# A mixture-of-experts stage on one Trainium2 core: the first expert product turned, its weights streamed per slot

## The chip, the cores and the metric

The kernel runs on one core of one Trainium2 chip, in one launch. The metric is the device time in microseconds; three runs of the kernel before took 3836.7 to 3844.87 us, with a median of 3841.38 us. A core has five engines that run their own instruction streams and meet at semaphores: PE (TensorE, matrix products), DVE (VectorE), ACT (ScalarE), POOL (GpSimd) and SP (SyncE, which here only issues DMAs). PE accumulates into PSUM, eight banks of 512 float32 per partition (`bank0` to `bank7`); everything else lies in SBUF, 128 partitions wide.

## The reference, cut to what matters

One layer of a graph transformer on 3125 nodes of 256 features, all in float32: three rounds of a relational graph convolution over 103,125 edges with 8 relations, a linear attention beside it, and a feed-forward part in which a router picks 2 of 8 experts for each node. The change is in the last part:

```python
xn = (xt - mu) * jax.lax.rsqrt(var + LN_EPS)
xe = xn[None, :, :] * ln_g[:, None, :] + ln_b[:, None, :]
h = jax.nn.gelu(jnp.einsum('end,edh->enh', xe, W1) + b1[:, None, :], approximate=False)
y = jnp.einsum('enh,ehd->end', h, W2) + b2[:, None, :]
sel = jnp.take_along_axis(jnp.transpose(y, (1, 0, 2)), top_idx[:, :, None], axis=1)
out = (weights[:, :, None] * sel).sum(axis=1)
```

W1 is 8 x 256 x 1024 (8 MB), W2 is 8 x 1024 x 256 (8 MB). The kernel doesn't compute all eight experts for each node: it sorts the 6250 chosen (node, expert) pairs by expert into 56 slots of 128 rows, each of one expert, and computes each slot once.

## The kernel before, in words

**Layers.** Three graph layers follow each other. In each, POOL issues one indirect DMA per tile of 128 edges (`gather`, L473, 806 a layer), which brings 128 rows of 256 features from `rows_dram` into one of 22 gather places, taken in two halves of 11. PE multiplies each tile with a one-hot matrix (L1293), DVE adds the result up (L987), and PE multiplies what was collected for 128 nodes with the relation weights (L1236). The one-hot matrices of 11 tiles are made by one DVE instruction (L958), and ACT copies the indices of the next 11 gathers into a ring (L554) once PE has finished the 11 tiles that used those places before: the 23rd gather of a layer waits for the first 11 tiles of PE.

**Start of the last layer.** DVE and PE wait there for `ffw_in`, the small parameters of the experts: SP loads `ln_g`, `ln_b` (L376, L377; one DMA per expert and vector, each of 256 single words), the router's weights and `b1` (L380). DVE then fills `bsel` (L948, L950) and makes the first one-hot matrices. After these loads SP starts on the part of W1 whose place in `arena` isn't in use (L389).

**Preparing the slots.** After the last layer DVE computes the routing: where each pair goes (`pos`) and which expert each slot has (`slot_exp`). POOL then scatters the normed rows into `xs_dram`, one indirect DMA for each tile of 128 nodes and choice (L507, 50 in all). Meanwhile all of W1 and W2 is brought into SBUF (L389, L391), PE works out `ln_b @ W1` for all experts (`fold`, L1387), DVE adds it to `b1` (L1112), and ACT and DVE multiply W1 by `ln_g` in place (L735, L1114, eight instructions of 128 x 1024 each). `b1` goes out to `b1_dram`.

**Slots.** A slot s on PE, in the order in which it is written (`slot`, L1415): four plus four transposes of the Gelu rows (L1423); `hidden` of slot s+1, four products of 128 x 512 with the rows as stationary side (L1411); two transposes of the rows of slot s+2 (L1430); the second product of slot s, eight products of 128 x 256 (L1438). Around it DVE adds the bias to the hidden rows (L1123), ACT applies Gelu (L749), DVE and ACT copy the turned rows back (L1130, L756), ACT copies the turned rows of the next input back (L740), and DVE adds `b2` (L1135). SP reads the slot's expert number, loads `b1` and `b2` of that expert into all 128 partitions (L405, 512 KB; L406, 128 KB), loads the rows (L401) and stores the result (L422). In float32 each product is two passes on PE, each with its own weight load, so the trace counts 8, 16 and 8 matmuls for L1411, L1438 and L1423 (a transpose is one pass).

**Combining.** When all slots are stored, POOL gathers the results back (L518) and DVE adds them to the nodes (L1152).

## Time and profile before

| | us |
|---|---|
| median of 3 runs | 3841.38 |
| the profiled execution | 3845.77 |
| its span, first to last instruction | 3844.0 |
| three graph layers, up to the last end of a layer on DVE | 3183.6 |
| routing, from there to the first scatter | 21.6 |
| scatter, to the first load of rows | 70.6 |
| slots, from the first load of rows to the end of the last second product | 491.4 |
| combining, to the end | 76.8 |

The profile is of one execution, on the only core. Each engine's work is shown by its busy time; an engine's idle time costs something only where that engine is the one that the others wait for. On the right of a line of the timeline stands how long the engine was idle before it, and what ended that. `DMA` rows give the time from issue to landing. Where a product has more than one form, the views leave its shape out.

### The profile page before, as it was taken

Reading aid. Unit: us, or ns where it says so; the run is one execution under the profiler, and the core shown is the slowest. Engines: PE = TensorE matmul, PEld = TensorE weight load, DVE = VectorE, ACT = ScalarE, POOL = GpSimd, SP = SyncE. Lnnn points to the kernel's source line nnn. Section 1 sums busy time; section 2 is a strip of 40 time slices with the busy share of each in tenths; the row PEclk is TensorE's granted clock in tenths of the full one; section 3 lists DMA queues with packets and bytes.
Section 4 is the critical chain, followed back from the end, with each engine's and each line's share of the span. In section 5 each row is a group of like instructions: output and inputs, shape, how many; then the busy total and the mean of one; then the engine's idle time right before and its main releaser. Section 6 shows DMA issues by size and latency. Waiting matters only on the chain.

```text
span 3844.0 us, 55574 instructions
## 1 busy us (share of the span) xinstructions
PE 3026.0 (79%) x15306; PEld 2475.6 (64%) x15307; DVE 1830.8 (48%) x3744; ACT 689.2 (18%) x1109; POOL 2399.1 (62%) x2536
## 2 busy tenths in 40 slices
PE   2888788888768888888888677877877884899991
PEld 2767667676657677776777566776766761566661
DVE  5455554554545555455454365565555542222222
ACT  0111111111111111111111122122222221222220
POOL 3777777777757777777776577777777755000005
PEclk9788988888978877788787788788878877899996
DMA  4333333433443333333333433333333325333334
GB/s 149 114 113 115 114 113 113 117 113 113 117 123 109 109 107 107 109 108 108 109 108 102 146 106 104 105 105 105 106 105 105 105 80 197 104 105 105 106 113 129
DMA packets 205784, 434.65 MB, mean 113 GB/s; under 512 B 51647, under 2 KB 115608, under 8 KB 205674
## 3 DMA queue, kind: packets, MB, share of 16 engines
q0 software_dynamic: 120864, 330.20, 30.0%
q1 hardware_dynamic: 81424, 102.07, 8.1%
q10 hardware_dynamic: 3386, 1.24, 0.1%
q14 instruction: 81, 0.66, 0.1%
q8 instruction: 29, 0.48, 0.1%
HBM read 398.24 MB, written 35.09 MB: 113 GB/s over the span
## 4 chain that ended last, share of the span: by engine, by line
POOL 46%; PE 22%; issue 21%; DMA 4%; DVE 3%; DVEq 1%; ACT 1%; SPq 1%; ACTq 0%; POOLq 0%
POOL arena L473 44%; PE bank L1293 7%; PE bank L1411 4%; PE bank L1438 4%; PE bank L1236 4%; DMA arena<-rows_dram,arena 2%; POOL xs_dram L507 1%; PE bank L1423 1%; POOL arena L518 1%; DMA hT_all<-in_L_ffn_b_dram 1%; PE bank L1231 1%; DVEq L973 1%; PE bank L1229 1%; DMA arena<-in_L_gnn_roots_dram 0%; DVE arena L987 0%
## 5 line engine op out<-in xcount | busy, mean ns | idle before, releaser
L473 POOL DMA_INDIRECT arena<-rows_dram,arena x2418 | 2289.9, 947 | 848.6 <-issue 783.2
L1293 PE MATMUL bank<-arena 128*128 128x128 f32 x9672 | 1756.4, 329 | 578.5 <-DVE arena L987 309.8
L1293 PEld LDWEIGHTS bank<-arena 128*128 128x128 f32 x9672 | 1526.3, 229 | 823.2 <-DVE arena L987 429.4
L987 DVE TENSOR_TENSOR arena<-arena,bank 128x256 f32 x2418 | 1019.2, 422 | 1385.6 <-PE bank L1293 1076.7
L1236 PE MATMUL bank<-arena 128*128 128x256 f32 x2400 | 612.6, 397 | 0.0
L1236 PEld LDWEIGHTS bank<-arena 128*128 128x128 f32 x2400 | 457.4, 203 | 52.0
L571 ACT COPY arena<-arena 128x1024 f32<-128x1024 f32 x150 | 300.8, 2053 | 607.1 <-DVE arena L928 308.1
L518 POOL DMA_INDIRECT arena<-ys_dram,pos x50 | 48.5, 969 | 511.0 <-DMA ys_dram<-arena 496.1
L958 DVE TENSOR_TENSOR arena<-bank,arena 128x1408 f32<-128x1408 f32 x222 | 355.9, 1604 | 15.4 <-issue 15.2
L1123 DVE TENSOR_TENSOR hT_all<-bank,hT_all 128x512 f32<-128x512 f32 x114 | 73.7, 687 | 342.6 <-DMA hT_all<-in_L_ffn_b_dram 284.8
L1411 PE MATMUL bank<-arena 128*128 x456 | 211.3, 607 | 11.7 <-issue 11.4
L1438 PE MATMUL bank<-arena,hT_all 128*128 x896 | 202.7, 380 | 0.0
L1438 PEld LDWEIGHTS bank<-arena,hT_all 128*128 128x128 f32 x896 | 166.2, 190 | 20.0
L554 ACT COPY arena<-arena 128x11 int32 (+1 forms) x222 | 44.4, 201 | 731.7 <-PE bank L1293 714.9
L936 DVE MEMSET arena<- 128x2048 f32 x75 | 132.4, 1765 | 41.6 <-issue 25.9
L1411 PEld LDWEIGHTS bank<-arena 128*128 128x128 f32 x456 | 83.2, 192 | 103.0 <-issue 102.7
L604 ACT ACTIVATE arena<-bank 128x256 f32<-128x256 f32 x50 | 19.2, 384 | 607.6 <-PE bank L1236 607.6
L1231 PE MATMUL bank<-arena 128*128 128x256 f32 x300 | 124.0, 554 | 0.0
L507 POOL DMA_INDIRECT xs_dram<-hT_all,pos x50 | 54.1, 1082 | 74.3 <-DVE pos L1101 59.3
L1231 PEld LDWEIGHTS bank<-arena 128*128 128x128 f32 x300 | 71.0, 261 | 44.7 <-issue 35.5
L749 ACT ACTIVATE hT_all<-hT_all 128x512 f32<-128x512 f32 x114 | 70.0, 630 | 99.5 <-DVE hT_all L1123 99.5
L1173 PE MATMUL bank<-ident,arena 128*128 128x128 f32 x200 | 49.8, 339 | 41.8 <-DVE arena L846 27.6
(188 smaller groups left out, 1100.6 us busy)
## 6 DMA issues: line engine op xcount, KB each, us to landing
arena<-rows_dram,arena POOLq DMA_INDIRECT x2418, 2.8
hT_all<-b_dram SPq DMA_DIRECT2D x58, 512.0 KB, 3.5
arena<-in_L_ffn_W_dram SPq DMA_DIRECT2D x16, 512.0 KB, 7.6
arena<-in_L_ffn_W_dram SPq DMA_DIRECT2D x8, 1024.0 KB, 13.6
arena<-xs_dram SPq DMA_DIRECT2D x59, 128.0 KB, 3.6
hT_all<-in_L_ffn_b_dram SPq DMA_DIRECT2D x58, 128.0 KB, 3.9
ys_dram<-arena SPq DMA_DIRECT2D x56, 128.0 KB, 1.7
rows_dram<-arena SPq DMA_DIRECT2D x50, 128.0 KB
```

What stands on the lines that cost most here:

```text
L473: nc.gpsimd.indirect_dma_start(out=gath[:, slot, :], out_offset=None, in_=rows_dram[l], in_offset=bass.IndirectOffsetOnAxis(ap=idx_ring[:, ...
L507: nc.gpsimd.indirect_dma_start(out=xs_dram, out_offset=bass.IndirectOffsetOnAxis(ap=pos[:, c, t:t + 1], axis=0), in_=hT_all[:, t, :], in_o ...
L518: nc.gpsimd.indirect_dma_start(out=back[b][:, j, :], out_offset=None, in_=ys_dram, in_offset=bass.IndirectOffsetOnAxis(ap=pos[:, c, g * TG ...
L571: nc.scalar.copy(aggst[:, k, :, :], agg[:, k, at:at + TC].rearrange("p (n r) -> p r n", r=REL)).then_inc(S["stage_full"], 1)
L936: nc.vector.memset(agg[:, :, at:at + TC], 0.0).then_inc(S["agg_zero"], 1)
L958: nc.vector.tensor_tensor(onehot[:, CH * half:CH * half + n, :], bank[IOTA_BANK][:, 0:WC].unsqueeze(1).to_broadcast([P, n, WC]), loc[:, ba ...
L987: nc.vector.tensor_tensor(acc, acc, bank[EDGE_BANKS[u % 3]][:, 0:KD * WC].rearrange("p (k n) -> p k n", k=KD), ALU.add).then_inc(S["tile_a ...
L1231: nc.tensor.matmul(o, hT[:, k * P:(k + 1) * P], wroot[:, k, :], start=False, stop=False)
L1236: m = nc.tensor.matmul(o, aggst[:, k, r, :], wrel[:, k, r * D:(r + 1) * D], start=False, stop=c == CALLS - 1)
L1293: mm = nc.tensor.matmul(bank[EDGE_BANKS[u % 3]][:, k * WC:(k + 1) * WC], gath[:, slot, k * P:(k + 1) * P], onehot[:, slot, :], start=True, ...
L1411: m = nc.tensor.matmul(bank[1 + h][:, :], xsT[c][:, k, :], w1a[:, k, bass.ds(e * HF + h * 512, 512)], start=k == 0, stop=k == KD - 1)
L1438: m = nc.tensor.matmul(bank[5 + c][:, 0:D], hTq[:, q, :], w2a[:, q, bass.ds(e * D, D)], start=q == 0, stop=q == HC - 1)
```

## The change

The first product of a slot is turned: the stationary side is now a 128 x 128 block of the expert's W1, the moving side are the slot's turned rows, 128 columns, so the result has the hidden units on the partitions. Sixteen products of 128 x 128 take the place of four of 128 x 512. ACT reads the result from PSUM in eight pieces of 128 x 128, adds `b1` as a bias per partition, applies Gelu and writes straight into `hTq`, the stationary side of the second product. The eight transposes of Gelu rows and their copies are gone. `ln_g` and `ln_b` are applied by DVE as it copies the turned rows back (`scaled_rows`, two instructions), so W1 needs no scaling and `b1` no folding: `fold`, L735, L1112, L1114, `bsel` and `b1_dram` are gone.

W1 no longer lies in SBUF as a whole. Each slot loads its expert's 1 MB into one of two buffers (`load_weights`, two DMAs of 512 KB). `b1` is loaded once, in eight DMAs of 1024 single words each (`b1c`), and these are part of `ffw_in`. `b2` is loaded once into all partitions. The last two slots are written out, so that no product of a 57th slot is made.

```diff
-FFW = 2 * EXP + 3
+FFW = 3 * EXP + 2
+        w2q = [carve(EXP * D) for _ in range(W2_LOW)]
+        b2_all = carve(EXP * D)
+        w1s = [carve(KD * HF).rearrange("p (k n) -> p k n", k=KD) for _ in range(2)]
...
             for e in range(EXP):
                 sp.dma_start(gcols[:, e, :], ln_g[e].rearrange("(k p) -> p k", p=P)).then_inc(S["ffw_in"], 16)
-                sp.dma_start(bcols[:, :, e], ln_b[e].rearrange("(k p) -> p k", p=P)).then_inc(S["ffw_in"], 16)
+                sp.dma_start(bcols[:, e, :], ln_b[e].rearrange("(k p) -> p k", p=P)).then_inc(S["ffw_in"], 16)
+                sp.dma_start(b1c[:, e, :], b1[e].rearrange("(q p) -> p q", p=P)).then_inc(S["ffw_in"], 16)
...
-            sp.dma_start(b1_sb[0:EXP, :], b1).then_inc(S["ffw_in"], 16)
...
+            def load_weights(s, c):
+                e = sp.value_load(slot_exp[0:1, bass.ds(s, 1)], min_val=0, max_val=EXP - 1)
+                for k in range(KD):
+                    sp.dma_start(w1s[c][:, k, :], W1[bass.ds(e, 1), k * P:(k + 1) * P, :].rearrange("o p n -> p (o n)")).then_inc(s_w1[c], 16)
...
+            def feed(i, more):
                 for c in range(2):
                     s = 2 * i + c
-                    sp.wait_ge(S["xs_turned"], s + 2)
-                    load_rows(s + 3, 1 - c)
+                    if more:
+                        sp.wait_ge(S["xs_turned"], s + 1)
+                        sp.dma_start(xs[c], slot_rows(xs_dram, s + 2)).then_inc(s_xs[c], 16)
+                        sp.wait_ge(S["hid_mm"], 2 * s + 2)
+                        load_weights(s + 2, c)
                     sp.wait_ge(S["out_back"], s + 1)
-                    load_bias(s + 2, c)
...
+            def gelu(n, c, turn):
+                e = act.value_load(slot_exp[0:1, bass.ds(n, 1)], min_val=0, max_val=EXP - 1)
+                if turn is not None:
+                    act.wait_ge(S["out_mm"], turn)
                 for h in range(2):
-                    act.wait_ge(S["hid_pre"], 2 * s + h + 1)
-                    nc.scalar.activation(hrow[:, h * 512:(h + 1) * 512], hrow[:, h * 512:(h + 1) * 512], ACT.Gelu).then_inc(S["hid_act"], 1)
+                    act.wait_ge(S["hid_mm"], 2 * n + h + 1)
+                    for q in range(HC // 2):
+                        m = nc.scalar.activation(hTq[c][:, h * HC // 2 + q, :], bank[1 + 2 * c + h][:, q * P:(q + 1) * P], ACT.Gelu,
+                                                 bias=b1c[:, bass.ds(e, 1), h * HC // 2 + q])
...
+            def scaled_rows(n, c):
+                e = dve.value_load(slot_exp[0:1, bass.ds(n, 1)], min_val=0, max_val=EXP - 1)
+                dve.wait_ge(S["xs_turned"], n + 1)
+                if not (isinstance(n, int) and n < 2):
+                    dve.wait_ge(S["hid_mm"], 2 * n - 2)
+                for k in range(KD):
+                    m = nc.vector.tensor_scalar(xsT[c][:, k, :], bank[0][:, k * P:(k + 1) * P], gcols[:, bass.ds(e, 1), k],
+                                                bcols[:, bass.ds(e, 1), k], ALU.mult, ALU.add)
...
+            def hidden(n, c, load):
+                pe.wait_ge(S["xs_back"], n + 1)
+                pe.wait_ge(s_w1[c], 32 * load)
+                for q in range(HC):
+                    o = bank[1 + 2 * c + q // 4][:, q % 4 * P:(q % 4 + 1) * P]
                     for k in range(KD):
+                        m = nc.tensor.matmul(o, w1s[c][:, k, q * P:(q + 1) * P], xsT[c][:, k, :], start=k == 0, stop=k == KD - 1)
...
+            def slot(i, more):
                 for c in range(2):
                     s = 2 * i + c
+                    if more or c == 0:
+                        hidden(s + 1, 1 - c, i + 1 + c)
+                    if more:
+                        turn_rows(s + 2, c, i + 2)
+                    outer(s, c)
```

The order of PE in the loop over slots, before (a slot of the odd half, up to its second product; L1423 the transposes of Gelu rows, L1411 `hidden`, L1430 the transposes of input rows, L1438 the second product):

```order
L1423 MATMUL bank3<-ident,hT_all 128x128 x3
L1420 REGISTER_ALU
L1423 MATMUL bank4<-ident,hT_all 128x128 [waits hid_back_s,hid_act]
L1423 MATMUL bank4<-ident,hT_all 128x128 x3
L1405 ISA
L1405 TENSOR_LOAD arena
L1405 ISA x2
L1406 REGISTER_ALU
L265 ISA [waits xs_back]
L1411 ISA [waits hid_pre]
L1411 MATMUL bank1<-arena 128x512
```

And the same place now (L1362 `hidden`, L1141 the transposes of input rows, L1368 the load of the expert's number for the second product, L1373):

```order
L1358 REGISTER_ALU [waits xs_back]
L1362 MATMUL bank1<-arena 128x128 [waits w1_in0]
L1362 MATMUL bank1<-arena 128x128 x7
L1362 MATMUL bank2<-arena 128x128 x8
L1141 MATMUL bank0<-ident,arena 128x128 [waits xs_in1,xs_back]
L1141 MATMUL bank0<-ident,arena 128x128
L1368 ISA
L1368 TENSOR_LOAD arena
L1368 ISA x2
L266 ISA [waits out_back]
L1373 ISA [waits hid_act]
```

The slot now begins with `hidden`; the transposes are gone, and the only load of the expert's number on PE stands ahead of the second product. `hidden` waits for the weights' DMA.

SP in the same loop, before (L422 the store, L404 the load of the expert's number, L405 and L406 the two biases):

```order
L422 DMA ys_dram<-arena 128x256
L404 ISA
L404 TENSOR_LOAD arena
L404 ISA x2
L405 ISA
L405 DMA hT_all<-b1_dram 128x1024
L406 ISA
L406 DMA hT_all<-in_L0_ffn_b2_dram 128x256
L401 ISA [waits xs_turned]
L401 DMA arena<-xs_dram 128x256
```

And now, from the same wait for the result to the next (L414 the store, L410 the rows, L396 the weights):

```order
L410 ISA [waits xs_turned]
L410 DMA arena<-xs_dram 128x256
L411 ISA
L394 ISA [waits hid_mm]
L394 TENSOR_LOAD arena
L394 ISA x2
L396 ISA
L396 DMA arena<-in_L0_ffn_W1_dram 128x1024
L396 ISA
L396 DMA arena<-in_L0_ffn_W1_dram 128x1024
L414 ISA [waits out_back]
L414 DMA ys_dram<-arena 128x256
```

The rows are now asked for ahead of the large loads, not behind them, and two loads of 512 KB from W1 stand where one of 512 KB and one of 128 KB stood.

## Rows read from the trace of the kernel before

**Rows 1.** The page's part 1: busy time, share of the span, instructions.
```profile
PE 3026.0 (79%) x15306; PEld 2475.6 (64%) x15307; DVE 1830.8 (48%) x3744; ACT 689.2 (18%) x1109; POOL 2399.1 (62%) x2536
```

**Rows 2.** Windows, slots: us, busy per engine, PE clock, DMA share, GB/s.
```profile
3600.00:3700.00 100.00, 97.15 (x402) 65.38 (x401) 27.34 (x47) 25.38 (x47) 0.00 (x0) 1.00 0.34 109
```

**Rows 3.** Lines of the slots: busy us, mean ns, idle before.
```profile
L1123 DVE TENSOR_TENSOR hT_all<-bank,hT_all 128x512 f32<-128x512 f32 x110 | 71.0, 687 | 283.9 <-DMA hT_all<-in_L_ffn_b_dram 279.8 <-PE bank L1411 4.0
```

**Rows 4.** Timeline of PE, one slot: start us, us, line.
```profile
3444.05 3.70 PE L1411 MATMUL bank<-arena 128*128 x8 [0.45 <-issue]
3447.58 0.38 PE L1430 MATMUL bank<-ident,arena 128*128 128x128 f32 x2
3447.80 3.62 PE L1438 MATMUL bank<-arena,hT_all 128*128 x16
3451.25 1.04 PE L1423 MATMUL bank<-ident,hT_all 128*128 128x128 f32 x8
3452.13 3.60 PE L1411 MATMUL bank<-arena 128*128 x8
```

**Rows 5.** Timeline of PE, first and last product of the slots.
```profile
3282.61 6.41 PE L1411 MATMUL bank<-arena 128*128 x8
...
3763.55 3.62 PE L1438 MATMUL bank<-arena,hT_all 128*128 x16
```

**Rows 6.** Timeline of PE in the graph layers: products of 128 x 128.
```profile
1063.34 1.50 PE L1190 MATMUL bank<-arena 128*128 128x128 f32 x12
1064.68 1.26 PE L1293 MATMUL bank<-arena 128*128 128x128 f32 x8
...
2500.20 3.84 PE L1293 MATMUL bank<-arena 128*128 128x128 f32 x28
```

**Rows 7.** Timeline, end of a second product and SP behind it.
```profile
3439.82 2.32 PE L1438 MATMUL bank<-arena,hT_all 128*128 x10
...
3442.77 0.35 SPq L422 DMA_DIRECT2D ys_dram<-arena  x1
...
3443.96 0.34 SPq L405 DMA_DIRECT2D hT_all<-b_dram  x1
...
3444.48 0.33 SPq L406 DMA_DIRECT2D hT_all<-in_L_ffn_b_dram  x1
```

**Rows 8.** DMA issues: at 3183.6 us, at 3184, all, at 3275.7; last number us to landing.
```profile
arena<-in_L_ffn_W_dram SPq DMA_DIRECT2D x1, 512.0 KB, 4.1
...
arena<-in_L_ffn_W_dram SPq DMA_DIRECT2D x2, 512.0 KB, 4.5
...
arena<-in_L_ffn_W_dram SPq DMA_DIRECT2D x16, 512.0 KB, 7.6
...
arena<-xs_dram SPq DMA_DIRECT2D x1, 128.0 KB, 2.0
```

**Rows 9.** Timeline of the scatter on POOL, and DVE beside it.
```profile
3228.21 6.50 POOL L507 DMA_INDIRECT xs_dram<-hT_all,pos  x1 [0.30 <-issue]
...
3229.21 5.37 DVE L1114 TENSOR_SCALAR arena<-arena 128x1024 f32<-128x1024 f32 x8
```

**Rows 10.** Timeline of PE, transposes of the first slot's rows.
```profile
3277.92 0.66 PE L1400 MATMUL bank<-ident,arena 128*128 128x128 f32 x2 [49.35 <-DMA arena<-xs_dram]
```

**Rows 11.** Timeline, start of the last layer; last row an early DMA of 896 words.
```profile
2136.74 0.94 POOL L473 DMA_INDIRECT arena<-rows_dram,arena  x1 [29.87 <-issue]
...
2146.32 0.47 SPq L377 DMA_DIRECT2D arena<-in_L_ffn_ln_b_dram  x1
...
2150.09 0.17 DVE L948 MEMSET arena<- 128x128 f32 x1 [17.28 <-DMA arena<-in_L_ffn_b_dram]
...
2160.93 0.20 ACT L554 COPY arena<-arena 128x11 int32<-128x11 int32 x1 [27.15 <-PE bank L1293]
...
2164.24 0.94 POOL L473 DMA_INDIRECT arena<-rows_dram,arena  x1 [0.30 <-issue]
...
25.90 0.40 ACTq L538 DMA_DIRECT2D win_dram<-arena  x1
```

## What the change should do to the time

> **What bounds the kernel now.** I read the page's busy times first: no engine is full over the span, PE with 79% and POOL with 62% come closest [rows 1], so the bound has to be looked for by stage. The windows over the slots show it: PE is busy for 97 of 100 us at the full clock while POOL does nothing [rows 2]. In the graph layers it is POOL, with a gather each 1.25 us (22 from 2136.74 to 2164.24) [rows 11]. The timeline of PE takes a slot apart [rows 4]: `hidden` 3.53 us to the next product, two transposes 0.22, the second product 3.45, eight transposes of Gelu rows 0.88, together 8.08. From the first `hidden` to the end of the last second product pass 3763.55 + 3.62 - 3282.61 = 484.6 us [rows 5]. 57 times 3.53 and 56 times (0.22 + 3.45 + 0.88) are 456.0, the slow first `hidden` adds 6.41 - 3.70 = 2.7, so some 26 us are waits. What they wait for stands with DVE's bias add: it sat idle 279.8 us for the `b2` load, which lies behind the `b1` load, and Gelu and the transposes follow it [rows 3]. Idle DVE costs nothing by itself; here it is late by about half a microsecond in every other slot.
>
> **The slots.** PE's `hidden` becomes 16 products of 128 x 128, in two passes each, 32 passes. Products of that form stand in the graph layers: twelve passes from 1063.34 to the next line's start at 1064.68 are 0.112 us each [rows 6]. So 32 x 0.112 = 3.58 us, as before. The other end is the long run of 28 passes in 3.84 us, 0.137 each, which has waits in it: 4.38 us. I take 0.112, because `hidden` has no waits between its passes. The eight transposes go (0.88), and the peeled end drops the 57th `hidden` and two turns. PE's sum: 56 x 3.58 + 54 x 0.22 + 56 x 3.45 = 405.6, with 2.7 for the slow start 408.3 us, if nothing waits.
>
> What is late next? ACT now has eight pieces of 128 x 128 per slot. Its 47 instructions of 256 to 512 columns took 25.38 us, 0.54 each [rows 2]; eight shorter ones are at most 4.3 us beside 7.2 of PE, and the second product that needs them comes a whole `hidden` later. DVE's mean is 27.34 / 47 = 0.58 [rows 2], so its two scaled copies lie beside the second product (3.45 us). Neither waits. The weights do come near. SP asks for those of slot s+3 only after the result of slot s is back and stored, since `out_back` stands ahead of them in its queue. From the end of the second product (3439.82 + 2.32 = 3442.14) to the issue of the store are 0.63 us, one plain issue is 0.52 (3444.48 - 3443.96), one with the expert's number ahead of it 1.19 [rows 7]. In the new order: store 0.63, rows 1.15, first weights 2.34, second 2.86. They are needed 7.25 us after PE turned to the next `hidden`, which is 0.16 before the modelled end: at 7.09. The last W1 burst shows what such a pair takes: the first 4.1 us, the first two 4.5 on average, so the second 4.9 [rows 8]. It lands at 2.86 + 4.9 = 7.76, or at 6.96 if it is as quick as the first. So it is between 0 and 0.67 us late. A delay of L is shared by two slots, since the next request starts from the end of an earlier second product: 0 to 0.34 a slot, 0 to 18 us in all. I take 0.2 for 54 slots, 11 us. The rows land 2.0 us after their issue [rows 8], at 3.15, and are wanted 3.4 us after the same end (3.58 - 0.16): just in time. A second small doubt is the load of the expert's number on PE: where PE's queue was empty it cost the 0.45 us ahead of L1411 [rows 4]. Now it stands behind `hidden`, and the queue should hold work; 0 to 0.45 a slot, I take 0. The stage: 408.3 + 11 = 419.3, a gain of 65.3 us.
>
> The Trainium skill, "DMA: Bandwidth & Descriptors", section "Anatomy of one DMA", gives a transfer about 2.0 us plus its bytes at 436 GB/s (fitted on DMAs that GpSimd issues). By that the megabyte would be there 4.4 us after the first issue, at 6.74, and nothing would be late: an estimate of 3760 us in place of 3771. The 4.9 us above speak against it, and this trace has no pair alone on the queue.
>
> **The first slot.** SP issues both row loads back to back, ahead of no bias loads. The first transposes start at 3277.92 as before and take 0.66 [rows 10]; the two scaled copies some 0.5 (an estimate from DVE's 0.58 for longer ones), the second pair 0.66 and `hidden` at about 3279.8, not at 3282.61: 2.9 us gained, 2 to 3.3 as bounds. The W1 pieces of slots 0 and 1 load during the scatter.
>
> **The scatter.** It is on the path: POOL issues 50 scatters, and the first row load waits for the last. All take 0.97 us but one, which took 6.50, from 3228.21 to 3234.71. DVE's scaling of W1 runs from 3229.21 to 3234.58 [rows 9]. The two ends agree within 0.13 us, so I read this as POOL standing while DVE works. The scaling goes, hence 6.50 - 0.97 = 5.5 us less; the other end is 0, if the queue behind the weight loads did it.
>
> The Trainium skill, "SBUF — State Buffer", section "Who interferes with whom", says that VectorE and GpSimd share a port pair as an exclusive lock. By that rule the term is the 5.5 us, and by a backlog of the queue it would be less, since W2 still loads. The trace agrees with the rule by the 0.13 us.
>
> That the scaling and the folding ahead of it are gone gives nothing by itself: they ended at 3234.58, 43 us before the first transposes at 3277.92 [rows 9, 10], covered by the scatter.
>
> **The start of the last layer.** This is what the change costs, far from where it was made. `ffw_in` now needs eight more loads, of 1024 single words each, in SP's queue among the others. DVE waits for it until 2150.09. POOL has meanwhile gathered from 2136.74 on and issues its 23rd gather at 2164.24, for which ACT copied the indices at 2160.93 to 2161.13, after PE's eleventh tile: 3.1 us of slack [rows 11]. From there POOL runs without a gap to the end of the layer, so any stall is lost for good. An `ln_b` load of 256 words takes 0.47 us of SP, and with its gap 0.51; an early DMA of 896 words took 0.40 to issue [rows 11]. So the eight cost between 8 x 0.44 = 3.5 and 8 x 2.05 = 16.4 us. I take 0.9 each, near the lower end, because that row is the nearer in size: 7 us. DVE saves 0.5 by `bsel`. Stall: 7 - 0.3 (the old `b1` load) - 0.5 - 3.1 = 3 us, with 0 and 12.5 as bounds.
>
> **Sum.** 65.3 + 2.9 + 5.5 - 3.0 = 70.7 us less than the profiled execution's 3845.8: 3775.1. That execution was 4.4 above the median of the runs, so the median to expect is 3771 us.
>
> **Rivals.**
> No weights late: the pair lands as quickly as its first half, the 11 us go, 3760 us. For it: no third load runs behind the pair here. Against it: 1 MB in 4.6 us would be as quick as anything in these rows. Chance 0.25.
> PE's passes at the slower pace: 0.137 us for each of the 32, 0.8 more a slot, 45 us, while the weights' 11 us vanish: 3805. For it speaks the row of 28, against it that the twelve ran at 0.112 from the first. Chance 0.12.
> Eight word loads as dear as their words (2.05 each): the stall is 12.5 in place of 3, 3780. Chance 0.08.
> Slower than before: the weights land as the 16 earlier W1 loads did, 7.6 us in the median [rows 8]. Then they are there at 2.86 + 7.6 = 10.46, 3.37 late, 1.69 a slot, 91 us in place of 11: 3851. It decides from a lateness of 3.0 us on, that is from 7.2 us per load. Against it: the code issues those 16 in two batches, one behind the other, and the two at the head of the second took 4.1 and 4.9. Chance 0.05.
> My forecast with part of the waits has the other 0.50.
>
> **Range and chances.** Lower end 3756, both unknown waits at nothing. Upper end: 3771 with the full 18 us of waits, 8 us more at the layer's start and part of PE's possible 25 us for the expert's number, 3804, which also just reaches the slow passes. Left out is the slower case and some of the doubts together. A measurement of this kernel tells a change from none from about 0.2% on, 8 us. Only a sum of misfortunes ends near it: faster 0.94, same 0.01, slower 0.05.
>
> **What would show it.** In the profile after: `hidden` and the next line 3.6 us apart, 7.3 to 7.5 us from slot to slot, PE over 95% busy. If PE idles ahead of `hidden` for a DMA from W1, the weights are late; if the slot is 8 us long without such a wait, the passes are slower than 0.112. All scatters at 0.97 us. POOL's 23rd gather of the last layer about 3 us later than its rate. A gap ahead of the second product would be the expert's number. The forecast is wrong if weights take over 5.5 us to land or if the last layer's start loses over 8 us.

## The result, and the profile after

The changed kernel takes 3826.65 us (median of 7 runs, 3822.05 to 3828.39) against 3836.7 of before on the same chip (7 runs): a ratio of 0.9968, 95% interval 0.9959 to 0.9978. It is faster, by 10 us and not by the 70 forecast; the time lies above the range of 3756 to 3804.

The page's busy times, as in [rows 1]:

```profile
PE 2961.1 (77%) x16126; PEld 2546.3 (67%) x16127; DVE 1752.7 (46%) x3667; ACT 683.9 (18%) x1322; POOL 2393.6 (63%) x2536
```

The window in the slots, as in [rows 2]: PE was busy for 97 of 100 us, now for 91, at the same full clock. PE has become less busy in this stage, not more.

```profile
3600.00:3700.00 100.00, 90.64 (x595) 81.18 (x593) 13.11 (x34) 26.22 (x93) 0.00 (x0) 1.00 0.45 148
```

The timeline of PE over two slots, answering to [rows 4] (start us, us, line; L1362 `hidden`, L1141 the transposes of input rows, L1373 the second product):

```profile
3447.77 3.73 PE L1362 MATMUL bank<-arena 128*128 128x128 f32 x32
3451.80 0.44 PE L1141 MATMUL bank<-ident,arena 128*128 128x128 f32 x2 [0.30 <-DMA arena<-xs_dram]
3452.96 3.71 PE L1373 MATMUL bank<-arena,hT_all 128*128 x16 [0.72 <-ACT hT_all L731]
3456.51 3.73 PE L1362 MATMUL bank<-arena 128*128 128x128 f32 x32
3460.29 0.41 PE L1141 MATMUL bank<-ident,arena 128*128 128x128 f32 x2
3461.37 3.72 PE L1373 MATMUL bank<-arena,hT_all 128*128 x16 [0.68 <-issue]
```

Forecast were 3.58 us from L1362 to L1141, 0.22 from there to L1373 and 3.45 to the next L1362. The rows show 4.03 and 3.78, then 1.16 and 1.08, then 3.55. Over the whole loop the means are 3.87, 1.11 and 3.55, and two second products lie 8.52 us apart: just as in the kernel before, where the mean was 8.52 too. The passes themselves keep the forecast pace, 0.112 us each. So the time taken out of PE's work came back as gaps. Against the forecast's 7.25 a slot is about 1.3 us too long: 0.9 of it lies ahead of the second product, 0.3 ahead of the turned rows, 0.1 inside the second product.

The page says of the second product whom it waited for: 20.3 of its 37.1 us are put down to Gelu (ACT, L731). For weights from W1 it hardly waits: PE's weight loads (PEld) of `hidden` sat idle for 3.1 us in all, 0.2 of them put down to that DMA.

```profile
L1373 PE MATMUL bank<-arena,hT_all 128*128 x896 | 207.6, 385 | 37.1 <-ACT hT_all L731 20.3
L1362 PEld LDWEIGHTS bank<-arena 128*128 128x128 f32 x1792 | 209.8, 193 | 3.1 <-DMA arena<-in_L_ffn_W_dram 0.2
```

First and last product of the slots, as in [rows 5]; the stage is 3742.07 + 7.07 - 3273.52 = 475.6 us (the last row holds two slots):

```profile
3273.52 8.55 PE L1362 MATMUL bank<-arena 128*128 128x128 f32 x64
...
3742.07 7.07 PE L1373 MATMUL bank<-arena,hT_all 128*128 x32
```

The start of the last layer, as in [rows 11]: first gather, the 22nd and the 23rd, and DVE's first one-hot matrices.

```profile
2134.26 0.94 POOL L463 DMA_INDIRECT arena<-rows_dram,arena  x1 [30.04 <-issue]
...
2155.52 3.16 DVE L930 TENSOR_TENSOR arena<-bank,arena 128x1408 f32<-128x1408 f32 x2 [24.88 <-DMA arena<-in_L_ffn_br_dram]
...
2160.51 0.95 POOL L463 DMA_INDIRECT arena<-rows_dram,arena  x1 [0.30 <-issue]
2166.56 0.94 POOL L463 DMA_INDIRECT arena<-rows_dram,arena  x1 [5.11 <-ACT arena L544]
```

Where the 17.9 us between the two profiled spans (3844.0 and 3826.1) are:

| stretch | before | after | difference | forecast |
|---|---|---|---|---|
| start to the first gather of the last layer | 2136.7 | 2134.3 | -2.5 | 0 |
| from there to the first scatter | 1068.5 | 1069.9 | +1.4 | +3.0 |
| first scatter to the first turned rows | 72.7 | 67.1 | -5.6 | -5.5 |
| first turned rows to the first `hidden` | 4.7 | 2.2 | -2.5 | -2.9 |
| slots | 484.6 | 475.6 | -8.9 | -65.3 |
| combining | 76.8 | 77.0 | +0.1 | 0 |

The first row is scatter between executions: in four later profiles with the same granted clock, of kernels with the old and the new code, it is 2134.1 to 2136.7. The second scatters as well: 1068.5 us here, 1066.0 in a later profile of a kernel with the same code up to there (experiment 8). Only the row of the slots is off by more than that.

### The profile page after: what moved, and what is told of

Same layout as the page of the kernel before. It is cut to its first block, busy times and chain, and to the rows that moved or that the text cites. A ratio compares the mean times of both kernels' runs of the same rounds, so it can differ in the third digit from the quotient of the medians.

```text
span 3826.1 us, 57998 instructions
## 1 busy us (share of the span) xinstructions
PE 2961.1 (77%) x16126; PEld 2546.3 (67%) x16127; DVE 1752.7 (46%) x3667; ACT 683.9 (18%) x1322; POOL 2393.6 (63%) x2536
## 4 chain that ended last, share of the span: by engine, by line
POOL 43%; PE 27%; issue 21%; DMA 3%; DVE 3%; DVEq 1%; ACT 1%; ACTq 1%; SPq 1%; POOLq 0%
POOL arena L463 40%; PE bank L1261 9%; PE bank L1373 5%; PE bank L1362 5%; PE bank L1204 5%; DMA arena<-rows_dram,arena 3%; POOL xs_dram L497 1%; POOL arena L508 1%; PE bank L1199 1%; DVEq L945 1%; PE bank L1197 1%; DVE arena L959 1%; PE bank L1141 0%; ACT arena L561 0%; ACT hT_all L731 0%
## 5 line engine op out<-in xcount | busy, mean ns | idle before, releaser
L1261 PE MATMUL bank<-arena 128*128 128x128 f32 x9672 | 1762.5, 330 | 574.1 <-DVE arena L959 309.3
L1261 PEld LDWEIGHTS bank<-arena 128*128 128x128 f32 x9672 | 1532.1, 229 | 818.1 <-DVE arena L959 438.8
L1204 PEld LDWEIGHTS bank<-arena 128*128 128x128 f32 x2400 | 454.4, 202 | 52.1 <-issue 0.9
L508 POOL DMA_INDIRECT arena<-ys_dram,pos x50 | 48.6, 972 | 499.5 <-DMA ys_dram<-arena 484.6
L1373 PE MATMUL bank<-arena,hT_all 128*128 x896 | 207.6, 385 | 37.1 <-ACT hT_all L731 20.3
L1373 PEld LDWEIGHTS bank<-arena,hT_all 128*128 128x128 f32 x896 | 165.4, 189 | 70.0 <-issue 49.4
L1362 PEld LDWEIGHTS bank<-arena 128*128 128x128 f32 x1792 | 209.8, 193 | 3.1 <-DMA arena<-in_L_ffn_W_dram 0.2
L1362 PE MATMUL bank<-arena 128*128 128x128 f32 x1792 | 210.1, 276 | 0.0
L731 ACT ACTIVATE hT_all<-bank,arena 128x128 f32<-128x128 f32 x448 | 127.6, 368 | 337.8 <-PE bank L1362 337.6
L1141 PE MATMUL bank<-ident,arena 128*128 128x128 f32 x312 | 74.5, 327 | 124.4 <-DMA arena<-xs_dram 80.1
L1089 DVE TENSOR_SCALAR arena<-bank,arena 128x128 f32<-128x128 f32 x112 | 40.8, 406 | 281.2 <-PE bank L1141 281.2
L1141 PEld LDWEIGHTS bank<-ident,arena 128*128 128x128 f32 x312 | 38.1, 159 | 145.1 <-issue 131.7
L1101 DVE TENSOR_TENSOR arena<-bank,arena 128x256 f32<-128x256 f32 x56 | 23.8, 425 | 199.2 <-PE bank L1373 199.2
```

Of the source, the lines that this page charges most:

```text
L731: m = nc.scalar.activation(hTq[c][:, h * HC // 2 + q, :], bank[1 + 2 * c + h][:, q * P:(q + 1) * P], ACT.Gelu, bias=b1c[:, bass.ds(e, 1), ...
L1141: m = nc.tensor.transpose(bank[b][:, k * P:(k + 1) * P], rows[:, k * P:(k + 1) * P], ident[:, :])
L1204: m = nc.tensor.matmul(o, aggst[:, k, r, :], wrel[:, k, r * D:(r + 1) * D], start=False, stop=c == CALLS - 1)
L1261: mm = nc.tensor.matmul(bank[EDGE_BANKS[u % 3]][:, k * WC:(k + 1) * WC], gath[:, slot, k * P:(k + 1) * P], onehot[:, slot, :], start=True, ...
L1362: m = nc.tensor.matmul(o, w1s[c][:, k, q * P:(q + 1) * P], xsT[c][:, k, :], start=k == 0, stop=k == KD - 1)
L1373: m = nc.tensor.matmul(bank[5 + c][:, 0:D], hTq[c][:, q, :], w2q[q][:, bass.ds(e * D, D)], start=q == 0, stop=q == HC - 1)
```

## Experiments

The runs came from three chips. One (runs e0, e5, e8 and e10; the kernel before takes 3842.45 us there) is as fast as in the result above. On the other two (e1 to e4: 5043.81 us; e7, e9 and e11: 5057.82 us) the graph layers took some 1200 us longer in every kernel (mean granted clock of PE 0.75 in place of 0.84), while the slots kept their times. Ratios are to the kernel before on the same chip, and the lengths of the stage (first `hidden` to the end of the last second product, from the timelines) can be compared across all three. The three distances below are means over the loop, from the starts of PE's first passes in each trace. The very first distance, 8.3 to 9.7 us, is left out, since two `hidden` lie in it:

| kernel | `hidden` to turned rows | to second product | to next `hidden` | stage |
|---|---|---|---|---|
| changed kernel | 3.87 | 1.11 | 3.55 | 475.6 |
| the same, run again (e0) | 3.85 | 1.11 | 3.55 | 475.2 |
| number first (e1) | 3.74 | 0.32 | 3.72 | 437.1 |
| rows and weights early (e2) | 3.57 | 0.22 | 3.46 | 406.9 |
| both (e3) | 3.57 | 0.22 | 3.46 | 408.0 |
| rows alone early (e8) | 3.62 | 0.22 | 3.50 | 412.0 |
| number twice (e7) | 3.84 | 1.77 | 3.71 | 519.2 |
| number twice, early (e9) | 3.57 | 0.22 | 3.46 | 406.8 |
| number three times, early (e11) | 3.57 | 0.68 | 3.56 | 437.7 |
| b1 out of the first loads (e4) | 3.83 | 1.11 | 3.55 | 474.9 |
| all edits (e5) | 3.57 | 0.22 | 3.46 | 406.8 |

**1. The number ahead of `hidden`.** PE reads the expert's number for the second product ahead of `hidden` and no longer behind the turned rows.

```diff
             def slot(i, more):
                     s = 2 * i + c
+                    e = pe.value_load(slot_exp[0:1, bass.ds(s, 1)], min_val=0, max_val=EXP - 1)
                     if more or c == 0:
                         hidden(s + 1, 1 - c, i + 1 + c)
                     if more:
                         turn_rows(s + 2, c, i + 2)
-                    outer(s, c)
+                    outer(s, c, e)
```

> Start: the changed kernel, 3826.65 us; in its profile a slot is 8.52 us on average where 7.25 plus waits was forecast. Of the difference 0.89 us lies between the turned rows and the second product (1.11 where 0.22 was forecast), 0.37 us ahead of the turned rows (3.95 after the start of hidden, where 3.58 was forecast). Edit: PE reads the expert's number for the second product ahead of hidden, not after the turned rows. Theory A (PE's sequencer is held by the wait for the rows, and only then works through the load of the number, 0.75 us from 3460.30 to 3461.06, and the waits): the 1.11 us become about 0.35, 54 x 0.75 = 40 us less, near 3786 us. Rival B (the second product waits for Gelu on ACT, as the profile names it): no change, 3826. Rival C (whatever goes here, the wait for the rows takes it up, since they come at a fixed distance from the end of the last second product): 3826 too, with the idle time now ahead of the turned rows.

Measured: 4990.14 us against 5043.81 of before, 0.9898 (0.9884 to 0.9912). The stage is 38.3 us shorter than in the changed kernel (437.1 us against 475.4, the mean of its two profiles); 40 were expected. The timeline of PE, and of SP (L414 the store, L410 the rows, L396 both weight loads):

```profile
4604.43 3.84 PE L1362 MATMUL bank<-arena 128*128 128x128 f32 x32
4608.36 0.44 PE L1141 MATMUL bank<-ident,arena 128*128 128x128 f32 x2
4608.76 3.72 PE L1372 MATMUL bank<-arena,hT_all 128*128 x16
4612.63 3.84 PE L1362 MATMUL bank<-arena 128*128 128x128 f32 x32 [0.16 <-DMA arena<-in_L_ffn_W_dram]
```

```profile
4605.26 0.36 SPq L414 DMA_DIRECT2D ys_dram<-arena  x1
4606.17 0.34 SPq L410 DMA_DIRECT2D arena<-xs_dram  x1
4607.46 0.85 SPq L396 DMA_DIRECT2D arena<-in_L_ffn_W_dram  x2
```

From turned rows to second product are now 0.40 us in this slot, 0.32 on average. So the second product was not waiting for Gelu; rival B falls. The page had named it, and the chain of waits of the changed kernel leads through it too (start, us, what; ACTq is ACT's sequencer):

```profile
3452.30 0.28 ACTq L725
3452.59 0.20 ACT hT_all L731
3452.78 0.18 issue
3452.96 3.71 PE bank L1373 x16
```

That Gelu belongs to the `hidden` just done, whose rows the next second product needs and not this one. C holds in a small part: in every other slot the rows are still late (here 3.93 us in place of 3.57; 3.74 on average), and now the weights are as well, 0.27 us a slot ahead of `hidden`. In the changed kernel the gap had hidden them.

**2. Rows and weights asked for one store earlier.** The edit is in SP's loop only. `store` waits for `out_back` and issues the store of the slot named; the last slot's store stands behind the loop, outside this cut:

```diff
                     if more:
                         sp.wait_ge(S["xs_turned"], s + 1)
                         sp.dma_start(xs[c], slot_rows(xs_dram, s + 2)).then_inc(s_xs[c], 16)
                         sp.wait_ge(S["hid_mm"], 2 * s + 2)
                         load_weights(s + 2, c)
-                    sp.wait_ge(S["out_back"], s + 1)
-                    sp.dma_start(slot_rows(ys_dram[0:SLOTS, :], s), orow[c]).then_inc(s_ys[c], 16)
+                    if not (isinstance(s, int) and s == 0):
+                        store(s - 1, 1 - c)
```

> Edit: SP stores the result of a slot one slot later, so that the rows and weights of slot s+2 are asked for during the second product of slot s-1 and not after its end; PE's order is untouched. Theory A (the late rows hold the sequencer; with the rows there it runs ahead, and the load of the number is hidden behind hidden's passes): both gaps go, 54 x (0.37 + 0.89 + 0.1) = 73 us less at most, near 3757 us; hidden to turned rows 3.58, turned rows to second product 0.22. Rival D (passes of 128 columns are so short that the queue behind the sequencer is empty at the turned rows whatever the rows do): only the 0.37 goes, 20 us less, near 3807 us, the 1.11 stays. Rival B (Gelu): at most 20 us less.

Measured: 4968.61 us, 0.9852 (0.9839 to 0.9865); stage 406.9, 68 us shorter, with PE's order of work untouched. The timeline of PE:

```profile
4602.96 3.73 PE L1367 MATMUL bank<-arena 128*128 128x128 f32 x32
4606.53 0.38 PE L1146 MATMUL bank<-ident,arena 128*128 128x128 f32 x2
4606.74 3.62 PE L1378 MATMUL bank<-arena,hT_all 128*128 x16
4610.20 3.73 PE L1367 MATMUL bank<-arena 128*128 128x128 f32 x32
```

3.57, 0.21 and 3.46: the forecast's slot of 7.25, without a gap. The load of the number still stands between the transposes and the second product, and costs nothing. The records of PE's sequencer show why; start and duration are the trace's, what each does is put in words. In the changed kernel, for the first slot of the timeline above (the last pass of `hidden` starts at 3451.22, so the next instruction could have started at 3451.34):

```
3449.345   42 ns  L1352 register, wait for xs_back
3451.797   51 ns  L1368 register            (the rows have landed, the first transpose starts)
3451.911  297 ns  L1368 load of the number
3452.267  151 ns  L1368 register
3452.649   37 ns  L266  wait for out_back
3452.744   51 ns  L271  wait for hid_act
3452.850   51 ns  L1373 register
3452.951  186 ns  L1373 first weight load of the second product
```

The sequencer was at L1352 with 17 passes of `hidden` still to run. Then it stood for 2.45 us until the rows were there, and everything behind that wait, 1.15 us of register work, came while PE had only two transposes to do. With the rows in time (here L1373 is the load, L1378 the second product):

```
4604.537   51 ns  L1357 wait for the rows
4604.870  348 ns  L1373 load of the number
4605.562   46 ns  L266  wait for out_back
4605.696   51 ns  L271  wait for hid_act
4605.802   46 ns  L1378 register            (0.72 us ahead of the first transpose)
```

The same work lies under the last passes of `hidden`. Theory A holds, D falls.

The changed kernel itself has a slot whose rows came in time, the second of the loop. SP issued them at 3286.76, they landed 2.2 us later, at 3288.94, and the transposes started at 3289.16, 3.57 us after `hidden`, as if nothing had been waited for:

```profile
3285.59 3.73 PE L1362 MATMUL bank<-arena 128*128 128x128 f32 x32
3289.16 0.38 PE L1141 MATMUL bank<-ident,arena 128*128 128x128 f32 x2
3289.97 0.48 PE L1373 MATMUL bank<-arena,hT_all 128*128 x1 [0.44 <-issue]
```

Still 0.81 us pass up to the second product, in place of 0.22, and 0.88 in the same slot of the second profile (e0). Rows that land just before they are wanted already lay the number bare.

**3. Both.**

> Both edits: the number read ahead of hidden, and rows and weights asked for one store earlier. Theory A: near the second run, 3755 us, since with the rows in time the number was hidden already. Rival D: the two add up, 20 + 40 = 60 us less, 3766 us, against 3807 in the second run. Rival B (Gelu): 3807.

Measured: 4958.93 us, 0.984 (0.9827 to 0.9853). The slots are as in the second run, 7.24 us; the stage is 408.0, the difference of 1.1 us lies in the first distance, which the table leaves out (9.73 and 8.60 us). The 9.7 us between the two medians are not from this stage: in the two profiles it begins at 4489.2 and 4466.2 us. Once the rows are in time, moving the number gives nothing.

**4. The dose.** The number is read twice in the changed kernel (e7), and twice (e9) and three times (e11) in the kernel of the second run. The edit for one more read:

```diff
             def outer(s, c):
+                pe.value_load(slot_exp[0:1, bass.ds(s, 1)], min_val=0, max_val=EXP - 1)
                 e = pe.value_load(slot_exp[0:1, bass.ds(s, 1)], min_val=0, max_val=EXP - 1)
```

> The changed kernel (rows asked for late), with PE reading the expert's number twice ahead of each second product. Theory A (once the late rows release PE's sequencer, whatever it has to work through is paid in full): the gap from turned rows to second product grows from 1.11 by 0.75 to 1.86 us in nearly every slot, the stage from 475 to 515 us, the time by about 40 us. Rival (Gelu or something else on the path, the number beside it): the gap grows by less than 0.3.

> The same double read in the kernel with rows and weights asked for one store earlier. There the sequencer began on the number 1.77 us ahead of the turned rows and was through at 4605.80, 0.73 us ahead of them, by the raw times of one slot. A second read costs it 0.75. Theory A: the slot stays at 7.24 to 7.30 us, the stage at 407 to 411 us; 40 us of work on the sequencer cost nothing here and 40 in the run beside it. Rival D (no lead over short passes): 7.24 + 0.75 = 8.0 us.

> Three reads of the number in the same kernel, to find the end of the lead. Theory A: the first two are covered, the third only as far as the two transposes reach, so that the gap ahead of the second product grows from 0.22 by 0.5 to 0.75 us: slots of 7.75 to 8.0 us, a stage of 435 to 450 us. If the lead were set by time and not by the passes still queued, it would be the same as with two.

Measured against 5057.82 us: 5085.57 us, 1.0049 (1.0034 to 1.0064); 4974.73 us, 0.9837 (0.9819 to 0.9854); 5005.82 us, 0.9899 (0.988 to 0.9918). Stages: 519.2, 406.8 and 437.7. The same extra read makes the stage 44 us longer where the rows are late and costs nothing where they are in time; a third one costs 31. Of the 44 us the gap accounts for 36 (0.66 a slot, where 0.75 was expected). The other 8 lie in five second products, which took 5.24 us and not 3.56: seven of their passes came 0.427 us apart and not 0.216, the pace of the lower clock level (1.2 GHz). From 4889 to 4893 us, inside one of them, the granted clock was 0.59; ahead of it PE had idled over a microsecond in each slot. The other changed kernels have no such pass in the loop. Timelines of e7 and e11:

```profile
4606.04 0.41 PE L1141 MATMUL bank<-ident,arena 128*128 128x128 f32 x2
4607.82 3.72 PE L1374 MATMUL bank<-arena,hT_all 128*128 x16 [1.37 <-ACT hT_all L731]
```

```profile
4603.97 0.38 PE L1146 MATMUL bank<-ident,arena 128*128 128x128 f32 x2
4604.66 3.72 PE L1380 MATMUL bank<-arena,hT_all 128*128 x16 [0.31 <-issue]
```

The first pair of rows is the clearest case of a misnamed releaser: the gap grew from 1.11 to 1.77 us because PE read a number twice, and the profile still says Gelu. The second is named "issue", as it should be. The changed kernel with the double read is slower than before: the margin of the change was that thin. The expectation for the third read says that a lead set by time would show as with two reads. That does not follow: all of `hidden`'s passes are of one length, so 17 passes and 1.9 us are the same here, and the run does not tell the two apart.

**5. The rows alone.** As the second run, but the weights stay behind the store:

```diff
                         sp.dma_start(xs[c], slot_rows(xs_dram, s + 2)).then_inc(s_xs[c], 16)
-                        sp.wait_ge(S["hid_mm"], 2 * s + 2)
-                        load_weights(s + 2, c)
                     if not (isinstance(s, int) and s == 0):
                         store(s - 1, 1 - c)
+                    if more:
+                        sp.wait_ge(S["hid_mm"], 2 * s + 2)
+                        load_weights(s + 2, c)
```

> Edit: as the second run, but only the rows are asked for ahead of the store of the slot before; the weights of slot s+2 stay behind that store, where the changed kernel has them. It asks what the weights alone cost in a slot of 7.25 us. By the prediction's term (a pair lands 0.67 us late at most, shared by two slots) the stage is 408 + 11 = 419 us, with waits of hidden for the weights. Rival, by the median of 4.2 us from issue to landing in the changed kernel's profile: the second of the pair is issued some 2.5 us after the start of hidden and lands at 6.7 to 6.9, ahead of 7.25; nothing waits, the stage is 408 us, as in the second run.

Measured: 3765.4 us, 0.9801 (0.9788 to 0.9814); stage 412.0. The answer lies between the two: slots of 7.33 on average, 5 us for the stage. From 3300 to 3650 us the waits of PE's weight loads for the weights' DMA (us in total, times, longest) are:

```profile
PEld bank L1368 <- DMA arena<-in_L_ffn_W_dram: 8.0, 25, 0.5
```

This is the term that the forecast put at 11 us, with 0 to 18 as bounds.

**6. b1 out of the loads that the last layer waits for.**

```diff
-FFW = 3 * EXP + 2
+FFW = 2 * EXP + 2
...
-                sp.dma_start(b1c[:, e, :], b1[e].rearrange("(q p) -> p q", p=P)).then_inc(S["ffw_in"], 16)
...
+                if q == HC - 1:
+                    for e in range(EXP):
+                        sp.dma_start(b1c[:, e, :], b1[e].rearrange("(q p) -> p q", p=P)).then_inc(S["b1_in"], 16)
```

> Edit: the changed kernel, but the eight loads of b1 in single words stand behind the loads of W2 after the last layer, with a semaphore of their own that ACT waits for before the first slot; so they are no part of what the last layer's start waits for. Theory: the 4.8 us for which POOL stood ahead of the 23rd gather of the last layer go, 3822 us, and nothing comes back. Rival: the slack is used up elsewhere or the issue of 1024 words delays the first weights and rows behind it on SP: between 3824 and 3830 us.

The expectation misplaces the loads: the loop over W2 begins with q = 5, 6, 7, so with `q == HC - 1` they stand behind its first three loads and run during the last layer, not after it. For the question it makes no difference, since nothing waits for them until the slots.

Measured: 5032.95 us, 0.9974 (0.9964 to 0.9984). Inconclusive: on this chip PE bounds the layers. POOL stands some 80 times in the last layer, mostly for ACT's copy behind PE, and ahead of the 23rd gather it stands 8.6 us with the edit and 8.7 to 9.4 in e1, e2 and e3 without it. The changed kernel itself has no run on this chip. The edit comes back in the next run.

**7. The changed kernel again, and all edits together.**

> The changed kernel unaltered, as the base for the others on the same chip. On the chip of the four runs before, the graph layers took some 1200 us longer in every kernel (PE's granted clock in them is a tenth lower), while the slots ran at the same pace as in the first two profiles. Expected: slots of 8.5 us, a stage about 9 us shorter than before's, ratio to before between 0.995 and 0.998 on either chip.

> Three edits together: number read ahead of hidden, rows and weights asked for one store earlier, b1's loads behind W2's. Expected: slots of 7.24 us, a stage of 408 us; against the changed kernel unaltered 70 us less for the slots and, where POOL bounds the graph layers, 4.8 us less for the last layer's start. Rival for the last part: on a chip where PE bounds the layers, the start of the last layer is hidden behind PE and moving b1 gives nothing.

Measured: 3829.46 us (3824.24 to 3832.47, 7 runs) for the changed kernel, 0.9967 (0.9956 to 0.9978); 3758.03 us (3755.97 to 3758.67, 5 runs) with all edits, 0.978 (0.9766 to 0.9793). So the best version is 84 us faster than before and 71 us faster than the change. Its window in the slots has PE busy throughout:

```profile
3400.00:3500.00 100.00, 100.00 (x695) 94.28 (x694) 15.92 (x42) 31.83 (x112) 0.00 (x0) 1.00 0.53 182
```

And the start of its last layer (DVE's first one-hot matrices, POOL's 22nd and 23rd gather):

```profile
2147.57 3.15 DVE L938 TENSOR_TENSOR arena<-bank,arena 128x1408 f32<-128x1408 f32 x2 [16.94 <-DMA arena<-in_L_ffn_br_dram]
...
2161.08 0.94 POOL L470 DMA_INDIRECT arena<-rows_dram,arena  x1 [0.30 <-issue]
2162.33 0.94 POOL L470 DMA_INDIRECT arena<-rows_dram,arena  x1 [0.30 <-issue]
```

POOL doesn't stand. In three executions with b1 among the first loads it stood 4.8, 2.5 and 3.5 us there (the changed kernel, the same again, rows alone). No pair of runs here differs in this edit alone on the chip where POOL bounds the layers.

**8. The scaling of W1, in the kernel before.** ACT scales both halves, DVE none:

```diff
-                nc.scalar.activation(w1a[:, 1, e * HF:(e + 1) * HF], w1a[:, 1, e * HF:(e + 1) * HF], ACT.Copy,
-                                     scale=gcols[:, e, 1:2]).then_inc(S["w_scaled"], 1)
+                for k in range(KD):
+                    nc.scalar.activation(w1a[:, k, e * HF:(e + 1) * HF], w1a[:, k, e * HF:(e + 1) * HF], ACT.Copy,
+                                         scale=gcols[:, e, k:k + 1]).then_inc(S["w_scaled"], 1)
...
-                nc.vector.tensor_scalar(w1a[:, 0, e * HF:(e + 1) * HF], w1a[:, 0, e * HF:(e + 1) * HF], gcols[:, e, 0:1], None,
-                                        ALU.mult).then_inc(S["w_scaled"], 1)
```

> The kernel before, with one edit: ACT scales all of W1, DVE none (sixteen instructions of 128 x 1024 on ACT, about 2.06 us each, 33 us, ready before the first hidden). If POOL stood 5.5 us in the scatter because DVE scaled beside it, the scatter of 6.50 us is gone, all 50 take 0.97, and the stretch from the first scatter to the first turned rows becomes 67.1 us in place of 72.7; the whole 5.5 us less. Rival, a backlog of the queue behind the weight loads: one scatter stays near 6.5 us and the time stays.

Measured: 3836.89 us against 3842.45, 0.9986 (0.9977 to 0.9995). The longest of the 50 scatters takes 1.0 us, where one took 6.50 [rows 9], and from the first scatter (3202.72) to the first turned rows are 67.2 us, where there were 72.7. The loads run as before (245 and 246 GB/s from 3205 to 3240 us), so it was no backlog of the queue: the stall was DVE's work beside POOL. The Trainium skill, "SBUF — State Buffer", section "Who interferes with whom", has the two engines lock their shared port against each other; the trace agrees, by the 6.50 us with DVE's work and 1.0 without. My price for ACT was wrong: 1.05 us each and not 2.06; nothing hung on it. ACT's scaling, and the first turned rows on PE:

```profile
3225.95 16.72 ACT L736 ACTIVATE arena<-arena 128x1024 f32<-128x1024 f32 x16 [41.93 <-PE bank L1385]
```

```profile
3269.96 0.66 PE L1398 MATMUL bank<-ident,arena 128*128 128x128 f32 x2 [44.05 <-DMA arena<-xs_dram]
```

## Why the prediction was wrong

**The step that failed** is the one sentence on the expert's number: "it stands behind `hidden`, and the queue should hold work; 0 to 0.45 a slot, I take 0". It cost 0.89 us a slot (1.11 where 0.22 was expected) and 0.10 more inside the second product, whose second pass then starts 0.32 us after the first and not 0.22. Over 54 slots that is 53 us of the 68.8 by which this stage (475.6) is above the best (406.8). The other 15.8 are the late rows, 0.30 a slot. The upper bound was wrong too: 0.45 us is the idle time behind the modelled end of the transposes in [rows 4], and part of the register work was covered by their passes. The full read, with the waits behind it, is 1.1 us.

The trace of before held the same sequence of events. In the slot of [rows 4] PE's sequencer stood at a wait among the transposes until 3442.94, and from there to the first weight load of `hidden` at 3444.04 it worked through the number and its waits, 1.10 us. The prediction put the 26 us of waits down to DVE's late bias, half a microsecond in every other slot. The timelines of before have 22 of the 26 between the first transpose of Gelu rows and `hidden`, where every other slot is 0.8 us longer (1.67 in place of 0.87), and in the slot of [rows 4] 0.6 us of it lie behind the last transpose, where the number is read.

**What let it through** is the step before: the rows would be "just in time", at 3.15 of 3.4 us. By that a wait of nothing was booked, and what stands behind the waiting instruction was not priced. In the timeline SP issues the rows 1.56 or 1.83 us after the start of `hidden`, every other time behind the branch of its loop; the forecast's 1.15 from the modelled end is 1.31 from there. They land 2.1 us later, at 3.7 or 3.9, and are wanted at 3.57. Until they land PE's sequencer stands, and it is that stop which lays the number bare. It would have done so on the forecast's own times too: 3.15 from the modelled end is 3.31 from the start of `hidden`, and in the slot whose rows landed at 3.35 the gap was 0.81 us. The runs show the two apart: the number away, 38 us less (e1); rows and weights early, 68 us less with the number where it was (e2); the rows alone early, 63 us less (e8). The gap ahead of the second product was named as a sign to look for, but not priced together with the rows.

**The other terms.** `hidden` in 32 passes: forecast 3.58, measured 3.57 between starts in the runs without gaps. So the rival with slow passes falls, and the one with weights 3.4 us late falls by 4.2 us to landing in place of 7.6 (112 loads of 512 KB in the profile after, median). The Trainium skill, "DMA: Bandwidth & Descriptors", section "Anatomy of one DMA", gives 2.0 us and the bytes at 436 GB/s, for one such load an estimate of 2.0 + 1.2 = 3.2 us; the trace has 4.2, with two loads back to back, and the trace decides. ACT's eight pieces lie beside PE, as said. The weights: forecast 11 us; in the changed kernel they cost next to nothing, 5 us in a slot of 7.3 (e8); in the queue order that the change has, with the number out of the way, 0.27 a slot, 14 us (e1). The first slot: -2.9 forecast, -2.5 measured. The scatter: -5.5 forecast, -5.6 measured, with DVE's work shown as its cause. The last layer's start: DVE began its first one-hot matrices 6.9 us later against the first gather than before (21.3 and 14.3 us), where 7 less 0.5 was said; seven of the eight loads of 1024 words took SP 0.47 us to issue, like one of 256, the first 0.94. The stall was 4.8 us in the profile and 2.5 and 3.5 in two others, forecast 3. With the rows moved and nothing else, so that the sequencer keeps its lead, the sum stands: 3771 forecast, 3765.4 measured. It is nearer than its parts, since the weights took 5 us and not 11.

**What stays open**: how early the rows must land for the number to be covered in full, since no run varied that; whether the sequencer's lead over short passes is a number of instructions or a time; what b1's place in the queue is worth by itself; and why the medians of e2 and e3, with equal slots, differ by 10 us.

## What to carry to other kernels

A wait that is only just met or just missed costs not its lateness alone. It also costs the register work behind it on that engine, as far as no queued work is left to cover it, since the engine's sequencer has lost its lead. So put loads of dynamic indices ahead of long work, and waits that may be late last. Where a profile names an engine as releaser, ask whose turn that signal was: here it was Gelu of the slot after.

## What the runs showed of the hardware

- Reading a number from SBUF into a register of PE and using it as an offset took 0.75 us of its sequencer (3460.30 to 3461.06 in the changed kernel, of which the load itself 0.30), and 1.1 us with two waits up to the first weight load. Two such reads were hidden behind 17 passes of 0.112 us, 1.9 us (e9); the third showed with 0.46 us (e11).
- The same program ran 1200 us longer on two of three chips, all of it ahead of the slots, where PE's granted clock was near 0.7 by the page in place of 0.8. The slots, at full clock, took 7.24 us to the hundredth on one of those two (e2) and on the third (e5).
- With gaps of 1.8 us in each slot (e7) the granted clock fell to its lower level (1.2 GHz) within five of 54 second products; each took 1.7 us longer for it.
- SP's queue alone moved 182 GB/s over the slots of the best version (e5), where the core moved 109 before.
